# A fused attention and expert layer on one core: PV in pairs, row maxima spaced by time, late token statistics taken at the start

## What is computed

```python
xn = _layernorm(x, axis=-1)
x = x + _L0_attn_ref(xn, Wqkv, Wout) + _L0_ffn_ref(xn, gate_w, w11, w33, w22, sw1, sw2, sw3)
# attention, H = 16, D = 16, seq 2048
q = q * cos + rotate_half(q) * sin ;  k = k * cos + rotate_half(k) * sin
scores = einsum('bhqd,bhkd->bhqk', q, k) * scale      # causal: -inf above the diagonal
out = einsum('bhqk,bhkd->bhqd', softmax(scores), v) @ Wout.T
# experts: sigmoid gate, 4 of 8 groups, 6 of 32 experts; silu(x w11) * (x w33) @ w22, weighted
```

## Time and profile before

| | us |
|---|---|
| median of 3 runs | 893.49 (893.37 to 894.62) |
| the profiled execution | 888.71 |
| its span | 886.7 |
| PE busy | 817.1 |
| DVE busy | 606.5 |
| ACT busy | 493.5 |
| mean granted TensorE clock | 0.977 |

### The profile page before, as it was taken

How to read it: one execution, slowest core, us unless ns; L and a number is a source line. 1 busy time by engine, 2 the same in 40 slices (tenths; PEclk the granted TensorE clock), 3 DMA queues, 4 the chain that set the end, 5 groups by cost and what they waited for, 6 DMA issues and landing times.

```text
span 886.7 us, 17207 instructions
## 1 busy us (share of the span) xinstructions
PE 817.1 (92%) x5089; PEld 442.3 (50%) x5090; DVE 606.5 (68%) x1187; ACT 493.5 (56%) x1214; POOL 505.4 (57%) x654
## 2 busy tenths in 40 slices
PE   4799987788989989999999999999999999999997
PEld 2366554233333433377888888873343333433444
DVE  2567787888887788755555555557788787888422
ACT  3456542154556557644444444457676767667762
POOL 3556660299989730066666666626878888820000
PEclk9799997699999999999999999999999999999999
DMA  9005554720000141058777877774585555520011
GB/s 235 1 32 175 172 176 150 190 74 18 1 19 1 36 108 37 1 135 258 220 220 245 235 233 231 141 145 76 72 170 90 72 89 72 89 32 1 13 37 48
DMA packets 82624, 96.43 MB, mean 109 GB/s; under 512 B 13660, under 2 KB 74076, under 8 KB 82524
## 3 DMA queue, kind: packets, MB, share of 16 engines
q0 software_dynamic: 19968, 31.47, 19.8%
q1 hardware_dynamic: 45672, 47.10, 18.2%
q10 hardware_dynamic: 16896, 16.78, 5.6%
HBM read 61.11 MB, written 33.82 MB: 107 GB/s over the span
## 4 chain that ended last, share of the span: by engine, by line
PE 77%; DVE 12%; issue 4%; DMA 2%; DVEq 2%; ACT 1%; POOLq 1%; POOL 1%; SPq 0%; ACTq 0%
PE bank L1208 14%; PE bank L1191 13%; PE vector_banks L1283 12%; PE vector_banks L1169 12%; DVE mpart L967 9%; PE bank L1300 6%; PE vector_banks L1061 5%; PE vector_banks L1082 4%; PE bank L1082 3%; PE bank L1061 2%; DMA xn_all<-wexp 2%; PE vector_banks L1228 2%; PE bank L1098 1%; PE vector_banks L1172 1%; PE bank L1194 1%
## 5 line engine op out<-in xcount | busy, mean ns | idle before, releaser
L967 DVE TENSOR_REDUCE mpart<-vector_banks 128x2 f32<-128x1024 f32 (+3 forms) x320 | 329.7, 1062 | 79.1 <-PE vector_banks L1169 48.8
L725 ACT ACTIVATE probs<-bank 128x512 f32<-128x512 f32 (+3 forms) x428 | 212.7, 539 | 123.9 <-PE bank L1191 62.9
L1191 PE MATMUL bank<-turned 108*128 108x512 bf16 (+3 forms) x640 | 201.4, 353 | 7.6 <-DVE turned L989 2.2
L1169 PE MATMUL vector_banks<-turned 96*128 96x512 bf16 (+3 forms) x640 | 185.0, 359 | 14.6 <-DVE mpart L967 13.7
L598 POOL DMA_INDIRECT turned<-normed_rows,tok_i x128 | 125.3, 979 | 122.2 <-PE vector_banks L1061 90.4
L613 POOL DMA_INDIRECT res<-expert_rows,slot_i x96 | 148.8, 1550 | 41.7 <-issue 28.4
L725 ACT ACTIVATE at_first<-bank 128x512 f32<-128x512 f32 (+3 forms) x212 | 105.6, 533 | 67.5 <-PE bank L1194 36.4
L1191 PEld LDWEIGHTS bank<-turned 108*128 108x128 bf16 x640 | 58.2, 97 | 164.0 <-ACT probs L725 71.8
L1283 PE MATMUL vector_banks<-xn_all,probs 128*128 x512 | 135.0, 386 | 3.9 <-issue 1.6
L1208 PE MATMUL bank<-probs,V 128*32 128x512 f32 (+3 forms) x856 | 102.3, 549 | 0.0
L1283 PEld LDWEIGHTS vector_banks<-xn_all,probs 128*128 128x128 f32 x512 | 87.2, 190 | 16.5 <-issue 8.6
(11 more groups left out here) (157 smaller groups left out, 963.0 us busy)
## 6 DMA issues: line engine op xcount, KB each, us to landing
expert_rows<-probs ACTq DMA_DIRECT2D x32, 512.0 KB, 4.2
term_rows<-at_first SPq DMA_DIRECT2D x96, 128.0 KB
turned<-term_rows SPq DMA_DIRECT2D x32, 384.0 KB, 4.9
xn_all<-wexp SPq DMA_DIRECT2D x32, 384.0 KB, 4.0
normed_rows<-xn_all SPq DMA_DIRECT2D x4, 512.0 KB, 5.9
turned<-normed_rows,tok_i POOLq DMA_INDIRECT x128, 3.8
out<-res SPq DMA_DIRECT2D x16, 128.0 KB, 1.7
res<-x SPq DMA_DIRECT2D x1, 1536.0 KB, 10.8
```

The source lines that it names most:

```text
L725: A(PT[v // 2 % 6][:, v % 2, 0:width], bank[A_BANK[step][0]][:, 0:width], ACT.Exp).then_inc(s["scalar_bank_read"], 1)
L967: V.tensor_reduce(mpart[:, t % TPC, 2 * j:2 * j + 2, p], ring[:, :, 0:w], AX.X, ALU.max).then_inc(s["vector_bank_read"], 1)
L1169: last = mm(ring[:, h, 0:w], q_turned(slice(0, KQ), 2 * j + h, t * P, P), k_turned(par, slice(0, KQ), 2 * j + h, p * CH, w), start=True, s ...
L1191: last = mm(ring[:, 0:CH - off], k_turned(parity(g), slice(0, KM), h, kb * P, P), q_turned(slice(0, KM), h, c * CH + off, CH - off), start ...
```

## The change

The diff, with the two new slices and what the prediction speaks of:

```diff
+MIDDLE, LAST = slice(QT4, 2 * QT4), slice(2 * QT4, NT)
@@ whole_order
-    def some(everything=False):
+    def some(eighths, everything=False):
         nonlocal at
-        at += 1
+        at += eighths / 8
@@ the walk over the key blocks
-        order.append(("st", g, c, kb, 0))
-        some()
-        order.append(("st", g, c, kb, 1))
-        some()
-        if len(pending) == 2:
-            values(pending.pop(0))
-        order.append(("st", g, c, kb, 2))
-        some()
-        order.append(("st", g, c, kb, 3))
-        some()
+        for when, step in [x for x in later if kb == 0 and x[1] == ("mt", g, c)]:
+            order.append(step)
+            later.remove((when, step))
+        for h in range(HG):
+            order.append(("st", g, c, kb, h))
+            some(6)
+        if kb % 2 == 0:
+            if len(pending) == 2:
+                values(pending.pop(0))
+                values(pending.pop(0))
+            some(16)
         pending.append((g, c, kb))
@@ sync
-            load_x(EARLY)
+            load_x(EARLY, "x_in")
 ...
+            load_x(MIDDLE, "middle_in")
+            load_x(LAST, "last_in")
             sp.dma_start(cos_sb[:, :, :], ...)
             sp.dma_start(sin_sb[:, :, :], ...)
-            sp.wait_ge(s["x_in"], 16)
-            load_x(LATE)
@@ scalar, the loop over tiles
+                if t == 0:
+                    act.wait_ge(s["var_ready"], 2)
+                    A(root[:, LATE], var[:, LATE], ACT.Sqrt).then_inc(s["root_ready"], 1)
                 proj_read(t, t % 2, t < 2)
 ...
                 if t == 1:
-                    act.wait_ge(s["var_ready"], 2)
-                    A(root[:, LATE], var[:, LATE], ACT.Sqrt).then_inc(s["root_ready"], 1)
-                if t == 2:
                     act.wait_ge(s["scales_ready"], 2)
-                for n in ((QT4, QT4 + 1, QT4 + 2) if t == 2 else (t + QT4,) if 2 < t < NT - QT4 else ()):
+                for n in ((QT4, QT4 + 1) if t == 1 else (t + QT4,) if 1 < t < NT - QT4 else ()):
                     norm(n)
@@ scalar, st
-                        if pvs >= 2:
-                            act.wait_ge(s["pv_done"], pvs - (h >= 2))
+                        if v // HG >= 3:
+                            act.wait_ge(s["pv_done"], v // HG - 2)
@@ vector
-            statistics(EARLY, 1)
+            statistics(EARLY, 1, ((EARLY, "x_in"),))
+            statistics(LATE, 2, ((MIDDLE, "middle_in"), (LAST, "last_in")))
 ...
-                if t == 1:
-                    statistics(LATE, 2)
```

More of the change, by code:

```diff
@@ L91, in due @@
         if at > a0:
-            upto = n0 + -(-(n1 - n0) * (min(at, a1) - a0) // (a1 - a0))
+            upto = n0 + int(-(-(n1 - n0) * (min(at, a1) - a0) // (a1 - a0)))
     return upto
@@ L163, in whole_order @@
             order.append(later.pop()[1])
-        order.append(("st", g, c, kb, 0))
-        some()
-        order.append(("st", g, c, kb, 1))
-        some()
-        if len(pending) == 2:
-            values(pending.pop(0))
-        order.append(("st", g, c, kb, 2))
-        some()
-        order.append(("st", g, c, kb, 3))
-        some()
+        for when, step in [x for x in later if kb == 0 and x[1] == ("mt", g, c)]:
[9 more added lines that the diff above has]
+            some(16)
         pending.append((g, c, kb))
-    some(True)
+    some(0, True)
     assert not later and not chain
@@ L383, in layer @@
         OVER_Y = (0, 1)
-        names = """x_in w_in tables_in w2_in xn_stored ident_made counts_made
+        names = """x_in middle_in last_in w_in tables_in w2_in xn_stored ident_made counts_made
             var_ready root_ready scales_ready xn_ready qk_ready xT_psum xT_ready proj_done rope_done proj_read act_ready hm_ready hT_psum hT_ready
@@ L403, in _, with load_x @@
         def _(sp):
-            def load_x(tiles):
+            def load_x(tiles, arrived):
                 sp.dma_start(res[:, tiles, :], x[tiles.start * P:tiles.stop * P, :].rearrange("(t p) d -> p t d", p=P)
-                             ).then_inc(s["x_in"], 16)
-            load_x(EARLY)
+                             ).then_inc(s[arrived], 16)
+            load_x(EARLY, "x_in")
             for dst, src, width in ((C_QK, wqkvT, 3 * D), (C_G, sw1T, D), (C_U, sw3T, D), (C_L, gateT, E)):
@@ L804, in shared_add, with statistics @@
                 V.tensor_tensor(row, row, bank[6][:, 0:D], ALU.add).then_inc(s["shared_added"], 1)
-            def statistics(tiles, part):
-                dve.wait_ge(s["x_in"], 16 * part)
-                for t in range(tiles.start, tiles.stop):
-                    V.bn_stats(stat[:, t, :], res[:, t, :])
+            def statistics(tiles, part, pieces):
+                for piece, arrived in pieces:
+                    dve.wait_ge(s[arrived], 16)
+                    for t in range(piece.start, piece.stop):
+                        V.bn_stats(stat[:, t, :], res[:, t, :])
                 dve.drain()
```

## The result

The changed kernel takes **908.58 us** (median of 4 runs, 903.67 to 912.03), the kernel before beside it 894.06 (893.37 to 895.28): a ratio of 1.0145 with a 95% interval of 1.0117 to 1.0173. By the medians it is 14.5 us slower, where 891.7 and a range of 877 to 899 were predicted. The profiled execution of the changed kernel took 912.03 us with a span of 910.0; it is the slowest of the four.

The account below looks back on a forecast made before the run. PE was taken as the bound, busy 92% of the span with 77% of the chain. Opening -6.3, stretches with strips +2.2, tail +2.3 and group 0 at 0 make -1.8: median 893.49 becomes 891.7 us, range 877 to 899.

Parts of the forecast that it names:

- Part 1: Opening: earlier statistics end PE's idle time and half clock before tile 4's turn; gain 6.3 us, next cycle at 41.95.
- It reaches the end in full: Whole kernel: the opening's 6.3 us gain lasts, as PE goes from tile to tile without a gap.
- Part 2: Attention: PV in pairs saves PE 0.20 us per pair, bounds 0.18 to 0.25, but ACT and DVE come into it.
- The rule quoted from the Trainium skill: PE in attention: changing tiling mode drains the TensorE, tiles of one mode run independently; alone it gives 15.6 us.
- 7 plain ones with `mt` at +0.1: Groups 1 to 3: seven plain two-block stretches with `mt` right before a pair, +0.1 us each, 0.7 in all.
- 10 with 128 and 512 columns at +0.1: Groups 1 to 3: ten stretches with these blocks, where the strips outlast PE, +0.1 us each, 1.0 in all.
- 11 with 384 and 256 at -0.2: Groups 1 to 3: eleven stretches with these blocks, where ACT is fast, -0.2 us each, -2.2 in all.
- costs nothing as long as it has to do 4.8 us in 5.8: Plain attention stretch: DVE has 2.36 us of buffered work over the pair, then idles at no cost.
- Group 0 ... I take 0: Group 0's 20 dense-strip stretches: up to +0.5 us each against PE's 0.2 saved; bounds -4 and +10, taken as 0.
- The tail, +2.3: Last 9 stretches, without strips: two at +0.6 us, five with output projections at +0.3, two narrow at -0.2; +2.3.
- the pair starves DVE: Rival, group 0 and `mt` waits: 20 stretches at +0.5, 11 waits growing 0.4; +12.6, 906 us; chance 0.12.
- 165 to 265 us takes longer: Sign in group 0's dense-strip window: if it takes longer, the dense part was underrated.

## Why the prediction failed, point by point

**Part 1 held as far as the opening goes.** The predicted times, and the kernel after in the timelines of DVE, ACT and PE: x in at 12.5, here at 12.72 at the latest; statistics done at 18.2, here 18.4; rope 0 not later than 19.54, here 18.89; no idle time ahead of tile 4's turn, here 36.08 behind 35.86. DVE first:

```profile
12.72 2.71 DVE L813 BATCH_NORM_STATS2 turned<-res 128x6 f32<-128x256 f32 x8 [1.66 <-DMA res<-x]
18.23 0.17 DVE L830 SCALAR_TENSOR_TENSOR turned<-turned 128x12 f32<-128x12 f32 x1
18.89 0.69 DVE L784 TENSOR_TENSOR turned<-vector_banks,turned 128x512 f32<-128x512 f32 x1 [0.49 <-PE bank L1084]
```

PE in the same kernel:

```profile
35.86 0.38 PE L1063 MATMUL bank<-ident,turned 128*128 128x128 f32 x2
36.08 0.38 PE L1063 MATMUL vector_banks<-ident,xn_all 128*128 128x128 f32 x2
...
42.56 0.38 PE L1063 MATMUL vector_banks<-ident,xn_all 128*128 128x128 f32 x2
```

From 36.08 to 42.56 are the 6.48 us of the sum. The gain is 48.26 - 42.56 = 5.7 and not 6.3, since tiles 0 to 2 came 0.6 later than in the earlier trace rows; alone it measured 6.4. The clock was 0.96 between 31 and 48 us, where 1.00 was expected from 31 on. "It reaches the end in full" held in the old order alone.

**Part 2, the price of a pair, held.** The second `pv` 0.87 to 0.95 behind the first: 0.88. Saving on PE 0.20, bounds 0.18 to 0.25: 0.24. The plain stretch 5.83: 5.80 to 5.93, and the experiments show ACT as its cause, as argued from the earlier trace rows. The rule quoted from the Trainium skill, "TensorEngine Tiling (Array Packing)", Key Properties, describes PE alone: with PE alone to count, such a stretch would have taken about 5.5 (5.68 less the 0.20 from the earlier trace rows), and it takes 5.44 where ACT is given half of its work, so the trace agrees with the rule, and the rule alone misses what stands behind PE.

**The steps that failed:**

1. *"7 plain ones with `mt` at +0.1 ... waits for DVE about as long as before."* It waits 1.60 us, not 1.0 (behind the experts the eight waits grew by 0.4 us in the mean), and the price in the stretch behind isn't the wait but what can follow it: the clock at its lower level over the pair. Three places cost 1.5 to 2.0 us each there (7.39 against 5.72, 7.26 against 5.72, 5.69 against 3.73; the last lies in the tail). Together they are 5.2 us, against +0.7 for all seven in the sum. Where the clock stayed up, the same three stretches took 5.70, 5.70 and 4.03. My sum had no term for the clock.
2. *"10 with 128 and 512 columns at +0.1", "11 with 384 and 256 at -0.2".* Here DVE's strips end last and a pair leaves DVE dry. Behind the experts the first kind measured +0.32 to +0.50 each, the second from -0.63 to +0.42, about 0 in the mean. I had written of DVE's gap that it "costs nothing as long as it has to do 4.8 us in 5.8", which holds for plain stretches alone; in one of 5.0 us it has no such room. With the maxima halved, the first kind fell by 0.4 to 0.5.
3. *"Group 0 ... I take 0", bounds -4 and +10.* Against the kernel with the statistics alone it was +6.9, within the bounds, but not by the mechanism that I weighed. The pair, at up to +0.5 in each of 20 stretches in my sum, cost 1.8 in all by one trace of each kernel (3.3 against the fastest trace of the old order); 5.9 came with the spacing alone, for which I had only "strips spaced by time spare some of the waits". I had costed the pairs and given the second half of the change no price of its own.
4. *The tail, +2.3*: too high for the order, and too low for this execution. With the clock at 1.00 in the tail the traces of the old order (with all exponentials) take 60.3 us to the end and those of the changed order 61.2, so the order costs 0.8 to 0.9. The 65.4 us of the changed kernel's trace go with a clock of 0.92. The old order has this too: 62.9 us at 0.94, in the kernel before with its gathers spaced.
5. *"It reaches the end in full ... all later steps hang on it."* With the old order it does, 6.4 us. With the new order the lead of 5.2 to 5.4 us stands up to mt(1,2) and isn't there in the medians (908.58 with it, 906.00 without). Its place was taken by things that don't hang on PE's steps: the stall at the gathers and the clock in the tail.

The outcome lies near the rival "the pair starves DVE" (906 us, chance 0.12), partly by luck. Its 0.4 us for the growth of an `mt` wait was right. Its dense part was 10 us, where 6.9 were measured, most of it not by the pair. It took the opening's 6.3 us as kept, and had neither the clock nor the stall. "165 to 265 us takes longer" was the sign named for it. The step that let me put it at 0.12 was the third: an unknown with bounds of -4 and +10 was carried at 0, and the range stopped short of its upper end, which alone would have reached past 899.

## What to carry to other kernels

Grouping instructions of one kind on the engine that is fullest saves its change-over, here 0.24 us a pair, but leaves every engine that it feeds without work for the length of the group; count what their buffers hold against that length in each kind of stretch, and not only in the one where they have most room. If a change does two things, price each alone, and run each alone first: here one half was worth 0.7%, the other cost 1.2%, and together they cost 1.45% and not 0.5%. Keep a wait that is known to be long away from the front of such a group. And before a difference between two profiled executions is put down to the change, look at what differs between traces with the same steps: here the clock behind a wait, the clock in the tail, and a stall.

## What was not expected of the hardware

Eight gathers in a row from POOL, one each 1.33 us, made ACT stand for 3.9 to 5.0 us and DVE for 2.7 to 3.2 with their data ready in the three traces of the old order with the early statistics; by the length of the piece 14 of 15 traces have it, in various shapes. With about 4 us between the gathers it is gone, and the kernel before is 0.64% faster by this alone, 1.2% together with the early statistics. It moves with the gathers, and perhaps with the packets of instructions that fall among them, which is inferred only; so a change far away can put it in or out.

The clock is the other one. Behind one and the same wait of 1.6 us of PE, with the same steps around it, it fell from 1.00 to its lower level in some executions and not in others, at 1.7 us each time.
